# Three routing groups instead of two for the experts of layer 2, and new slots for what is laid beside them

## The reference

```
gate_probs = softmax(x1 @ Wg + bg)                      # [B, S, 8]
topk_p, topk_i = top_k(gate_probs, 2); topk_p /= sum(topk_p)
comb = sum(one_hot(topk_i, 8) * topk_p)
h = gelu(einsum('bsd,edf->bsef', x1, W1) + b1)          # F = 512
y = einsum('bsef,efd->bsed', h, W2) + b2
out = layernorm(x1 + einsum('bse,bsed->bsd', comb, y)) * g2 + be2
```

## Time and profile before

| | us |
|---|---|
| median of three runs | 5564.1 |
| the three runs | 5554.41, 5564.1, 5571.5 |
| the profiled execution | 5564.1 |
| its span | 5562.2 |
| TensorE busy | 5141.9 (92%) |
| VectorE busy | 3941.6 (71%) |
| ScalarE busy | 2741.6 (49%) |
| GpSimd busy | 1365.6 (25%) |

### The profile page before, as it was taken

The page is one execution under the profiler, slowest core; times in us unless marked ns, Lnnn a source line. Parts: engine busy times, 40 slices in busy tenths (PEclk is TensorE's granted clock), DMA queues, the critical chain, the costliest instruction groups (busy, mean ns, idle before and its releaser), DMA issues. The chain is left out here.

```text
span 5562.2 us, 106818 instructions
## 1 busy us (share of the span) xinstructions
PE 5141.9 (92%) x41620; PEld 2665.9 (48%) x41620; DVE 3941.6 (71%) x6689; ACT 2741.6 (49%) x4626; POOL 1365.6 (25%) x1069
## 2 busy tenths in 40 slices
PE   6999997787999999899999989899999999997999
PEld 2343433344567777773332349433433334335676
DVE  7889995774677777777998954678778787864312
ACT  4777775221233333336786866455454444542333
POOL 0120110220122322322112214245344443440000
PEclk7999998887999999999999989999999999998999
DMA  4211210002111101111122113000000000001000
GB/s 92 49 34 33 44 22 12 0 0 60 38 35 28 34 19 30 33 24 32 28 39 39 43 53 87 29 17 16 13 13 20 13 13 9 13 16 35 5 5 8
DMA packets 146408, 156.99 MB, mean 28 GB/s; under 512 B 48756, under 2 KB 93092, under 8 KB 145492
## 3 DMA queue, kind: packets, MB, share of 16 engines
q1 hardware_dynamic: 141304, 141.06, 11.6%
q0 software_dynamic: 4096, 8.40, 0.5%
q10 hardware_dynamic: 504, 0.69, 0.1%
HBM read 117.35 MB, written 36.49 MB: 28 GB/s over the span
## 5 line engine op out<-in xcount | busy, mean ns | idle before, releaser
L4144 DVE TENSOR_REDUCE wide_max_parts<-wide_p 128x2 f32<-128x1024 f32 x496 | 595.4, 1220 | 132.5 <-PE wide_p L4113 120.5
L838 ACT ACTIVATE attn_w<-l_p 128x512 f32<-128x512 f32 x1024 | 548.7, 597 | 192.5 <-DVE l_p L1284 116.5
L2643 PE MATMUL caus_p<-caus_x_one,big 128*128 128x129 f32 x4608 | 638.1, 285 | 0.0
L684 DVE TENSOR_REDUCE l_max_parts<-l_p 128x2 f32<-128x1024 f32 x512 | 602.3, 1219 | 45.1 <-PE l_p L658 41.0
L2727 ACT ACTIVATE big<-caus_p 128x512 f32<-128x512 f32 (+3 forms) x768 | 345.5, 489 | 548.8 <-PE caus_p L2629 401.7
L684 DVE TENSOR_REDUCE rot_max_parts<-rot_p 128x2 f32<-128x1024 f32 x488 | 574.5, 1219 | 54.9 <-PE rot_p L658 51.4
L2643 PEld LDWEIGHTS caus_p<-caus_x_one,big 128*128 128x128 f32 x4608 | 589.1, 198 | 35.9 <-issue 2.7
L4421 PE MATMUL wide_p<-arena 64*128 64x512 f32 x2048 | 530.9, 597 | 0.0
L4559 ACT ACTIVATE attn_w<-wide_p 128x1024 f32<-128x1024 f32 x342 | 350.0, 1023 | 333.2 <-PE wide_p L4421 331.9
L4352 POOL TENSOR_TENSOR big<-big,attn_w 128x1024 f32<-128x1024 f32 x128 | 333.1, 2603 | 392.4 <-PE wide_p L4113 380.4
L684 DVE TENSOR_REDUCE caus_max_parts<-caus_p 128x2 f32<-128x1024 f32 (+2 forms) x360 | 340.4, 956 | 24.2 <-PE caus_p L658 15.9
(11 more groups left out here) (667 smaller groups left out, 8970.3 us busy)
## 6 DMA issues: line engine op xcount, KB each, us to landing
arena<-q_parts SPq DMA_DIRECT2D x576, 32.0 KB
arena<-k_parts SPq DMA_DIRECT2D x576, 32.0 KB
arena<-inverse_rows SPq DMA_DIRECT2D x64, 256.0 KB
l_q_stack<-q_parts SPq DMA_DIRECT2D x279, 32.0 KB
l_k_stack<-k_parts SPq DMA_DIRECT2D x279, 32.0 KB
q_parts<-arena SPq DMA_DIRECT2D x8, 768.0 KB, 3.6
k_parts<-arena SPq DMA_DIRECT2D x8, 768.0 KB, 3.6
moe_in<-const_zero_tiles SPq DMA_DIRECT2D x2, 2496.0 KB, 15.1
```

The lines of the kernel that those rows point to most:

```text
L684: self.nc.vector.tensor_reduce(self.max_parts[:, 2 * p:2 * p + 2, n, half], pair[:, :, 0:self.width(n, half)], AX.X, ALU.max).then_inc(*se ...
L838: self.nc.scalar.activation(self.exps[t % len(self.exps)], bank, ACT.Exp).then_inc(*self.exped.up())
L2643: mm = nc.tensor.matmul(outs[o % 2][:, nq % 2 * (C + 1):(nq % 2 + 1) * (C + 1)], exps[h % 2][:, kb, nq * P:(nq + 1) * P], x_one[b % 2][:, ...
L4144: self.nc.vector.tensor_reduce(self.max_parts[:, :, n, h], side, AX.X, ALU.max).then_inc(*self.maxed.up())
```

## The change

The 16 token tiles of the second group become two groups of 8. The third group takes over the room of the second in `attn_w` and the constants loaded for it; its logits wait for the second's last step. Each has its logits, pieces, counts and places, three a slot instead of four, from slots 0 and 14, and its scatters, one a slot, from slots 14 and 28. Gate rows move to slots 3, 7, 11, 15, 33, 37, 49 and 53. Gathers are one a slot throughout; the four combines of the first group, the tail and the next stage's first steps take new slots counted from the end of group 0, and `beside` is longer with the number of tiles. A third buffer pair and a third clearing DMA come with the third group (a loop over `ROUTED`, unchanged in the code).

```
--- before.py
+++ after.py
@@ -2772,7 +2772,7 @@
 
 
 E2, FF = 8, 512
-ROUTED = ((0, 16), (16, 16))
+ROUTED = ((0, 16), (16, 8), (24, 8))
 PER_EXPERT = FF // P + 2 * FF
 
 
@@ -2990,8 +2990,9 @@
         self.nc, self.inp = core.nc, core.inp
         self.gates = st.sbuf("gates", [P, core.n_batch * NT, E2])
         self.router = Router(st, E2)
-        rooms = [core.big[:, 0:2 * T], core.attn_w[:, 3 * BANK:4 * T]]
+        rooms = [core.big[:, 0:2 * T]] + [core.attn_w[:, 3 * BANK:4 * T]] * 2
         self.routes = [Route(st, g, self.router, rooms[g], self.gates) for g in range(len(ROUTED))]
+        self.routes[2].fixed_loaded = self.routes[1].fixed_loaded
         self.w = core.arena[:, 0:E2 * PER_EXPERT].rearrange("p (e w) -> p e w", e=E2)
         self.w_loaded = st.sem("expert_w_loaded")
 
@@ -3742,24 +3743,24 @@
     def lay(first, steps, at_once=1):
 
         for i, step in enumerate(steps):
-            beside[min(first + int(i / at_once), len(beside) - 1)].append(step)
-
-    route = routes[1]
-    pieces = [("gate_piece", 1)] * Route.GATES
-    pieces[Route.BEFORE_EXP:Route.BEFORE_EXP] = [("route_exp", 1)]
-    lay(0, [("logits", 1)] + pieces, 4)
-    lay(7, [("counts", 1)])
-    lay(8, [("place_piece", 1)] * Route.PLACES, 4)
-    lay(11, [("scatter", 1, s, n) for n in range(route.n) for s in range(2)], 4 / 3)
-    for c, first in enumerate((2, 6, 10, 14, 37, 41, 45, 49)):
+            beside[min(first + i // at_once, len(beside) - 1)].append(step)
+
+    for g, first in ((1, 0), (2, 14)):
+        route = routes[g]
+        pieces = [("gate_piece", g)] * Route.GATES
+        pieces[Route.BEFORE_EXP:Route.BEFORE_EXP] = [("route_exp", g)]
+        lay(first, [("logits", g)] + pieces, 3)
+        lay(first + 9, [("counts", g)])
+        lay(first + 10, [("place_piece", g)] * Route.PLACES, 3)
+        lay(first + 14, [("scatter", g, s, n) for n in range(route.n) for s in range(2)])
+    for c, first in enumerate((3, 7, 11, 15, 33, 37, 49, 53)):
         lay(first, [("gate_row", c), ("none",), ("biases", c)])
-    done, chunk = routes[0].n_out + LAG, 2 * back.size
-    gathers = [("gather", c, s, i) for c in range(len(back.chunks)) for s in range(2) for i in range(back.size)]
-    lay(done + 1, gathers[0:2 * chunk], 2)
-    lay(done + chunk + 1, gathers[2 * chunk:])
-    for c, first in enumerate((6, 10, 20, 28)):
-        lay(done + 1 + first, [("combine", c)])
-    first = done + chunk + 4
+    done = routes[0].n_out + LAG
+    lay(done + 1, [("gather", c, s, i) for c in range(len(back.chunks)) for s in range(2)
+                   for i in range(back.size)])
+    for c in range(len(back.chunks)):
+        lay(done + 2 * back.size * (c + 1) + 4, [("combine", c)])
+    first = done + 2 * back.size * 2 + 5
     steps = tail.steps(0)
     lay(first, steps + [("narrow",)])
     lay(first + len(steps) + 1, early, 2)
...
+                        routes[2].top.begin_on_sp()
...
-                    pe.wait_ge(*routes[1].counts_read.at(1))
+                    pe.wait_ge(*routes[2].counts_read.at(1))
...
+                    g = args[0]
+                    if g == 2:
+                        v.wait_ge(*routes[1].owned.at(1))
+                    routes[g].logits_on_dve(v, side[:, i, :])
...
-                        pool.wait_ge(*routes[1].owned.at(1))
+                        pool.wait_ge(*routes[2].owned.at(1))
```

More of the change, by code:

```diff
@@ L3862, in _ @@
                 elif kind == "logits":
-                    routes[args[0]].logits_on_dve(v, side[:, i, :])
+                    g = args[0]
+                    if g == 2:
+                        v.wait_ge(*routes[1].owned.at(1))
+                    routes[g].logits_on_dve(v, side[:, i, :])
                 elif kind == "gate_piece":
```

## The result

| | before | after |
|---|---|---|
| median, us | 5563.64 | 5590.57 |
| lowest and highest | 5552.2, 5571.5 | 5584.83, 5600.15 |
| profiled execution, us | 5564.1 | 5581.52 |

The ratio is 1.0054, interval 1.0042 to 1.0065: 30 us slower, 23 to 36. Forecast was 5592. So the time came out as forecast. The traces show that not all the terms behind it did, and that part of the agreement is luck; the kernel before, profiled again, shows how much hangs on one profile.

What follows compares the result with a forecast made beforehand. TensorE, busy 5141.9 of 5562.2 us, was taken as the bound. First stretch +24.7, second +4.9, third -2.8 and clearing +1.4 sum to +28.2 on 5564.1: forecast 5592 us, own range 5583 to 5602, stated range 5578 to 5604.

Steps and rivals of the forecast that it cites:

- first stretch: Routed expert stage, slots 0 to 51 before and 0 to 60 after: 121.40 us before, forecast to grow by 24.7.
- Padding: Routed experts: seven more tiles, each done in full whatever it holds, cost 12.5 us, plus 0.8 for turning them.
- the lost cover: Third stretch: without one up product between second key projection and its values, 0.8 us turns into waiting.
- Rival (a): Padding only: new neighbours, exponential and double VectorE slot hide behind TensorE's lag; +15.5 us, 5580; chance 0.14.
- Neighbours in the one-bank ring: First stretch: bias products or gate rows behind turn-ins wait for ScalarE's bank copy, six for one: 5.2 us.
- The second exponential: First stretch, slots 1 and 15: table loads and exponential delay tiles' weight copies; 2.1 us, bounds 0 and 3.9.
- Second stretch: Slots 61 to 73 after, VectorE's combines and norms: +4.9 us from combine, bank neighbour and clock fall.
- Third stretch: Slots 74 to 86 after, beginning the next stage: two tiles fewer, less lost cover, -2.8 us (-8.5 to 0).
- Rival (c): The last stretch shrinks to its busy work, -20.6 us, and earlier pauses hide: 5560; chance 0.05.
- The third clearing: Start of earlier expert stage: 0.46 MB more zeros delay the last expert weight, +1.4 us, bounds 0 and 4.
- rival (b): Each of some eight new pauses brings low TensorE clock, about 13 us more, 5606; chance 0.13.
- What was said to prove it wrong: First stretch growing by less than 20 us, or the last shrinking by more than 6.

Runs made afterwards that it cites:

- the two looks: The kernel before, unedited, profiled two more times: first stretch 133.2 and 135.2 us, the three stretches together 226.2 and 229.7 us.
- again: The kernel after, unedited, measured a second time: ratio to before 1.0049 (1.0033 to 1.0065).
- before_look_1: The kernel before, unedited, the first of its two extra profiles: first stretch 133.2 us, three stretches 226.2 us.
- pad_only: The kernel before with seven more empty sorted tiles in its second group, old slots kept: ratio to before 1.0019 (1.0010 to 1.0028).
- no_neighbours: The kernel after with gate rows moved so neither they nor bias products stand right behind a turn-in: ratio to before 1.0034 (1.0021 to 1.0046).
- combine_moved: The kernel after with the third combine at slot 72 instead of 69: ratio to before 1.0034 (1.0024 to 1.0044).
- all_three: The kernel after with gate rows off the turn-ins, third combine three slots later, clearing transfers behind the weights: ratio to before 0.9981 (0.9972 to 0.9990).
- clear_late_before: The kernel before with its two clearing transfers issued behind the earlier expert stage's weights: ratio to before 0.9968 (0.9956 to 0.9980).
- no_second_exp: The kernel after with the second and third groups' exponentials replaced by Identity, needing no table load: ratio to before 1.0033 (1.0023 to 1.0043).
- clear_late: The kernel after with its clearing transfers issued behind the earlier expert stage's weights and ramps: ratio to before 1.0003 (0.9991 to 1.0014).

## Why the prediction was right, and where it was not

**The base.** Forecast: +28.2 us on an execution of 5564.1. The step that was weak is taking that profile's first stretch as the kernel's: "120.33 of 121.40 us busy" describes one execution, and five others of the same order have 131 to 135 us. Against the two looks the stage grew by 21.4 and 17.9 us, not by 32.0, and the earlier stage by about 1. So against them the traces explain 19 to 23 us; against the forecast's own profile they show 33.6 (32.0 and 1.6). The ratios say 27 (18 to 36) and 30 (23 to 36), between the two. The 4 to 11 us missing against the looks I can't place: stages that the change does not touch differ between executions by as much (the attention between the two expert stages took 1745.4 us in the profile of after, 1756.9 in "again", 1752.8 in before_look_1). By neither account do the parts add up to 28.2, so that 5592 met 5590.57 is partly luck.

**Padding** (12.5 for seven tiles, 0.8 for turning them, 0.8 for the lost cover): 14.1 forecast. pad_only, which has the first two of these and not the third, shows 13.5 in its stage for 13.3. The cover's wait is seen in the kernel after: 1.32 us before the values' products (L4104 there) for 0.42, +0.9. Right, and the largest part. Rival (a), padding only, is refuted: no_neighbours and combine_moved take real time away.

**Neighbours in the one-bank ring** (5.2): all six pauses came, 0.81 to 1.21 us each, 5.8 in all, net of the one before 4.9. Right as a wait. Moving them away gave 9.3, since 1.7 came back from the clock, 1.3 from the cover told at no_neighbours, and some 0.5 has no row.

**The second exponential** (2.1, bounds 0 and 3.9): the wait before tile 17 was 1.18 (1.3 forecast), but that before tile 3 was 1.93 instead of 0.3. Sum 3.1. Taking it away gave 3.1 as well, but by other parts: 2.6 of these waits, and the rest from what no one row shows, while 0.55 stayed. The mis-sized term is slot 1: 1.4 us for 0.3. ScalarE's timeline of the kernel after there:

```profile
3303.92 1.14 ACT L3657 ACTIVATE big<-moe_p,big 128x128 f32<-128x128 f32 x4 [3.98 <-PE moe_p L3646]
3304.93 0.60 ACT L3622 COPY big<-moe_p 128x512 f32<-128x512 f32 x1
3305.55 1.28 ACT L2891 ACT_TABLE_LOAD   x1
3306.85 0.26 ACT L2891 ACTIVATE attn_w<-attn_w 128x64 f32<-128x64 f32 x1
3307.12 1.28 ACT L3657 ACT_TABLE_LOAD   x1
```

and VectorE's:

```profile
3307.14 0.22 DVE L2902 TENSOR_REDUCE attn_w<-attn_w 128x8 f32<-128x64 f32 x1 [3.38 <-ACT attn_w L2891]
3307.39 0.20 DVE L2905 RECIPROCAL attn_w<-attn_w 128x8 f32<-128x8 f32 x1
3308.11 0.43 DVE L3634 COPY big<-arena 128x516 f32 x1 [0.52 <-issue]
```

The chain is the one named for slot 15: gelus, bank copy, load, exponential, then VectorE's next piece and behind it the weight copy, which ends at 3308.54, and tile 3 starts at 3308.59. There are no down products yet in slots 0 and 1 (they run two tiles behind), so TensorE has less work ahead of tile 3 to cover it with than ahead of tile 17; in no_neighbours one gate row more in slot 2 takes 0.63 us off this wait. The Trainium skill (ScalarE: Activation LUTs, What ACT_TABLE_LOAD costs) adds about 1.38 us of draining to a load. These rows do not have it: 1.28 us of load start 0.02 us after the copy before them and end 0.02 us before the exponential.

**Second stretch** (+4.9): +3.6 measured. The wait before tile 71 was 3.44 (3.3), a fall of the clock followed (0.72 over 6 us, which is 0.50 over the 3.4 us from 3475.6), and combine_moved took 3.4 of it back: the double VectorE slot was the cause. The forecast overlooked that this stretch now has three turn-ins for four (slots 63, 67 and 71 for 52, 56, 60 and 64), 0.4 us less. Too large was the neighbour in slot 71, 1.1 forecast: its pause is 0.68, and with the combine moved the stretch is at 30.77 with it in place, 0.1 to 0.2 from the looks' 30.9.

**Third stretch** (-2.8): -2.8 against the first profile, -1.4 and -2.8 against the looks; look 1 (62.2) is the one without a fall of the clock there, which the kernel after and the other two have. Rival (c), a last stretch that shrinks to its work, is refuted by this: the maxima still wait 1.32 us each. **The third clearing** (+1.4): the wait for the last weight grew from 10.05 to 11.58 (+1.5), or from 10.2 in the looks (+1.4).

**The clock, rival (b)**: 13 us more, from falls behind eight new pauses. One fall came in the first stretch (slots 10 and 11) and one behind tile 71, 3.4 us at 0.50 each, at most 1.7 us of work; the third, in the last stretch, the kernel before has too. Refuted in its size.

**What was said to prove it wrong** did not happen: the first stretch grew by 31.3, or by 17.5 to 19.5 against the looks. On that basis, "less than 20 us" was met. So the forecast of the time stands and its account of the first stretch, 24.7, does not: against the looks it is 18.5. There the pauses without a named cause are fewer in the new order (3.8 us in the kernel after: 0.28, 0.40, 1.20 and 1.94; 7.5 and 8.3 in the looks), and less of the stretch is at the lower clock (11.6 us for 15.3 and 18.7). The two make 5.5 to 8 us, about what the forecast is too high by.

## What to carry to other kernels

Profile the kernel before more than once ahead of pricing a change of half a per cent: a stretch in one profile can be 12 us from its length in five others. A large transfer that nobody needs soon costs what stands behind it in the queue, here 17.5 us of one stage for one place in the issue order, more than what the regrouping's new slots cost (11.5 in the stage by the two moves of all_three, and 3.1 for the exponential). Before splitting a sort into more groups, count the padding first, since it was 13.5 us of the change, and the best order tried (all_three) still had a stage 10.1 us above clear_late_before's.

## What the runs showed that was not expected

**Pauses of several engines at once.** In before_look_1 the bias products (L3713) end at 3415.1, and VectorE's addition, which waits for them, starts at 3418.81; its timeline shows nothing else in those 3.7 us:

```profile
3418.81 0.69 DVE L3723 TENSOR_TENSOR x_mid<-moe_p,x_mid 128x512 f32<-128x512 f32 x1 [5.37 <-DMA arena<-caus_max_lo]
3419.53 0.43 DVE L3633 COPY big<-arena 128x516 f32 x1
```

ScalarE, whose up products (L3645) ended at 3416.2, starts their gelus at 3420.36. The releaser that the row names has no part in this stage. GpSimd's gathers go on at their pace until 3418.82 and then pause for 1.72 us too, so the four engines don't stop at one moment. The pauses come near the same slots in all executions of one order (22, 25, 29 and 44 to 49 before; 30 to 33 and 45 to 48 after), and once, in the forecast's profile, they were missing up to slot 52. What holds the engines stays open: no run here took a suspect away.

**Pause and clock.** The third stretch of before_look_1 is full of pauses (45.10 us busy of 62.16) and has a clock of 1.00, while in the first stretch of the kernel after a fall to 0.50 came 2.5 us behind the end of the 0.81 us pause at slot 9. In the same order, combine_moved has its fall 2.4 us behind the pause of 0.93 at slot 5, no_second_exp 1.9 us behind that of 0.92 at slot 17, and clear_late, with all six of these pauses, has none in the first stretch; the three kernels without the neighbours have none either. The length of one pause alone does not tell whether the clock falls. The Trainium skill (TensorE: Matmul & The Clock Gate, the table of advice) ties the fall to long gaps between bursts; the row before tile 71 agrees (3.44 us, then 0.72), the one at slot 9 does not.
